# Contiguous copies, transposes as matmuls, and a coefficient moved to GpSimd in a metaformer block

## Time and profile before

| | us |
|---|---|
| median of the runs | 225.13 |
| the profiled execution | 225.83 |
| its span, first to last instruction | 223.9 |
| TensorE busy | 199.1 (89%) |
| ACT busy | 127.7 (57%) |
| DVE busy | 124.9 (56%) |
| GpSimd busy | 51.6 (23%) |

### The profile page before, as it was taken

The page is one execution under the profiler, slowest core; times in us unless marked ns, Lnnn a source line. Parts: engine busy times, 40 slices in busy tenths (PEclk is TensorE's granted clock), DMA queues, the critical chain, the costliest instruction groups (busy, mean ns, idle before and its releaser), DMA issues.

```text
span 223.9 us, 6080 instructions
## 1 busy us (share of the span) xinstructions
PE 199.1 (89%) x2674; PEld 103.9 (46%) x2674; DVE 124.9 (56%) x231; ACT 127.7 (57%) x207; POOL 51.6 (23%) x54
## 2 busy tenths in 40 slices
PE   7769688799994977659899999999999999999992
PEld 3546478453352857656234344444444444444430
DVE  0594076937949697699843643355433455333554
ACT  2349942014436725738887667866678666687630
POOL 5190393008599960040021000000000000000000
PEclk9999999999999599988999999999999999999998
DMA  6991000000000000000008852540706416071001
GB/s 213 272 260 32 3 3 6 4 0 3 0 3 1 0 3 3 6 3 3 0 12 194 195 144 48 138 97 3 187 0 140 97 41 148 3 180 54 3 0 47
DMA packets 6601, 14.27 MB, mean 64 GB/s; under 512 B 2736, under 2 KB 4144, under 8 KB 5680
## 3 DMA queue, kind: packets, MB, share of 16 engines
q1 hardware_dynamic: 6576, 13.89, 25.4%
HBM read 12.71 MB, written 1.18 MB: 62 GB/s over the span
## 4 chain that ended last, share of the span: by engine, by line
PE 76%; DVE 12%; ACT 7%; issue 3%; POOL 1%; DVEq 0%; POOLq 0%
PE psum L730 25%; PE psum L712 25%; PE psum L555 7%; PE psum L432 2%; PE psum L529 2%; PE psum L565 2%; PE psum L616 1%; DVE place L1063 1%; PE psum L662 1%; PE psum L515 1%; DVE place L1007 1%; DVE st L1003 1%; PE psum L584 1%; PE psum L475 1%; ACT hid L881 1%
## 5 line engine op out<-in xcount | busy, mean ns | idle before, releaser
L712 PE MATMUL psum<-tok,w1s 128*64 128x512 f16 x512 | 60.8, 381 | 1.2 <-ACT hid L881 0.5
L1186 DVE SCALAR_TENSOR_TENSOR term<-psum,sm,wide 128x512 f32<-128x512 f32 x32 | 24.0, 751 | 55.1 <-PE psum L730 52.6
L881 ACT ACTIVATE hid<-psum,b1p 128x512 f32<-128x512 f32 x64 | 38.5, 699 | 15.1 <-PE psum L712 14.8
L712 PEld LDWEIGHTS psum<-tok,w1s 128*64 128x64 f16 x512 | 27.5, 110 | 36.1 <-issue 8.8
L730 PE MATMUL psum<-hid,w 128*64 128x512 f32 x128 | 29.0, 592 | 0.0
L881 ACT ACTIVATE w1f<-psum,b1p 128x512 f32<-128x512 f32 x32 | 19.5, 687 | 15.2 <-PE psum L712 14.9
L1191 DVE TENSOR_TENSOR x<-x,term 128x512 f32<-128x512 f32 x32 | 22.1, 692 | 1.1
L881 ACT ACTIVATE w1g<-psum,b1p 128x512 f32<-128x512 f32 x32 | 19.6, 712 | 0.3
L555 PE MATMUL psum<-h_pad,tap_bd 64*64 64x512 f32 x144 | 15.9, 590 | 0.0
L730 PEld LDWEIGHTS psum<-hid,w 128*64 128x64 f32 x128 | 9.0, 137 | 14.9 <-issue 9.0
L730 PE MATMUL psum<-w1f,w 128*64 128x512 f32 x64 | 15.1, 592 | 0.0
(11 more groups left out here) (147 smaller groups left out, 287.5 us busy)
## 6 DMA issues: line engine op xcount, KB each, us to landing
wide<-gate_store SPq DMA_DIRECT2D x14, 512.0 KB, 6.4
xs<-in_x SPq DMA_DIRECT2D x2, 512.0 KB, 3.9
w1f<-in_W SPq DMA_DIRECT2D x2, 512.0 KB, 10.0
block_out<-x SPq DMA_DIRECT2D x4, 256.0 KB, 6.2
wide<-gate_store SPq DMA_DIRECT2D x2, 384.0 KB, 5.6
hid<-in_W1T SPq DMA_DIRECT2D x1, 512.0 KB, 10.5
w<-in_W SPq DMA_DIRECT2D x1, 512.0 KB, 11.8
sm<-in_small SPq DMA_DIRECT2D x1, 407.0 KB, 7.8
```

The lines of the kernel that those rows point to most:

```text
L712: mm = pe.matmul(h_bank(tile)[side * H:(side + 1) * H, :], w1s[:, part, e, k * P + side * H:k * P + (side + 1) * H], tok[:, pair, half, b, :],
L881: act.activation(hid_of[u % 4][:, B2 * k + b, :], h_bank(tile), ACT.Gelu, bias=b1p[:, e * KT + k:e * KT + k + 1]).then_inc(gelu_ready, 1)
L1186: dve.scalar_tensor_tensor(term[:, u % 2, :], y_bank(u), b2t[:, e:e + 1], gate_b[part][:, e % (E // 2), :], ALU.add, ALU.mult).then_inc(te ...
```

## The change

1. The ACT copies `keep_dw`, `keep_xd` and `keep_back` no longer rearrange what they copy. `keep_xd` and `keep_back` copy a bank as it lies; `keep_dw` writes runs of eight values. The rearrangement is done by TensorE: `dct_over_w` and `windows` write their results to PSUM with eight f32 values between neighbouring columns, `to_frequencies` reads its stationary operand with that distance, and `inverse_over_kh` reads its own with a distance of 16. The channels lie in another order in x's and x1's columns (`by_side`), and the cosine matrices for that axis have their columns or rows permuted.
2. The transposes `windows`, `places`, `heads` and `to_frequencies` are 32 quarter matmuls with the identity instead of eight 128x128 transposes, and each raises its semaphore once, at its end, where it did so after each half. `times_wv` waits for both copied banks, where it began with the first.
3. The low branch's coefficient is applied to its input: GpSimd multiplies `xd` by `coef` into a new tile `low_in` (`scale_low_in`, four operations of 512 columns for the two pairs), and `low` reads it. The bias, times `coef`, is a new tile `coef_bias` (one operation at the start) which GpSimd adds to `rest` (one more operation for each bank in `rest_ahead`, four in all). `mix_branches` on DVE is then one contiguous addition for each bank, where it was an operation with bias and coefficient and a rearranging addition.
4. The order of all engines is new (`TURN`, `UPS`, `DOWNS`, `GELUS`, `ADDS`). On TensorE `gram_matrices(0)` comes before `conv_in(1)`, `conv_in(0)` before `dct_over_w(1)`, `heads(0)` before `conv_out(1)`, and pair 0's inverse transform before `low(1)`; `down` of unit 0 comes after three `up`. On DVE `residual(0)` comes before `mix_branches(1)`. On GpSimd `weights_of_first` comes after the two `scale_low_in`.
5. Functions `other_*` can share a copy between ACT and DVE; `SHARED` is zero for all, so none issues anything. The gates are stored in pieces of 64 values where it was 128.

```
 TURN = {
+    "scale_low_in": (1, 2), "router_weights": (3, 4), "keep_router_weights": (5, 6), "weights_of_first": (3, 11),
+    "dct_over_h": (1, 2), "square_columns": (1, 2), "dct_over_w": (5, 8), "windows": (6, 10), "conv_in": (7, 12),
+    "keep_dw": (3, 8), "keep_xd": (4, 10), "gelu_in": (7, 11), "norm_columns": (1, 3), "places": (9, 13),
+    "keep_xt": (9, 12), "join": (4, 6), "rest_ahead": (5, 8), "high": (7, 9), "gram_matrices": (11, 15),
+    "gram_times_w": (14, 16), "norms": (17, 18), "mask_gram": (7, 9), "taps": (19, 22), "logits": (20, 24),
...
+    "gelu_out": (18, 22), "conv_out": (23, 28), "project": (26, 30), "exponent": (16, 20), "heads": (27, 33),
+    "times_wv": (29, 35), "keep_y": (19, 23), "low": (31, 37), "mask_mix": (20, 22), "keep_yt": (21, 25),
+    "to_frequencies": (32, 39), "inverse_over_kh": (34, 41), "keep_back": (24, 28), "keep_half": (26, 29),
+    "square_tokens": (27, 36), "mix_branches": (21, 24), "inverse_over_kw": (36, 42), "high_part": (30, 42),
+    "tokens": (38, 44), "residual": (23, 26), "norm_tokens": (25, 29), "keep_tokens": (31, 49), "features": (43, 58),
+    "low_part": (10, 12), "router": (40, 54), "route": (27, 32), "gates_to_rows": (52, 61), "shares": (28, 33),
...
+UPS = (45, 46, 47, 49, 50, 51, 53, 55, 57, 59, 60, 62)
+DOWNS = (48, 56)
+GELUS = (32, 33, 34, 37, 38, 39, 40, 43, 44, 46, 47, 50)
+ADDS = (34, 35)
...
 def dct_over_w(p):
-                    mm = pe.matmul(slot(p, 1)[rows_of(b), by_half(cp, side)], dh[p][rows_of(side), by_half(cp, b)], dct_w[rows_of(side)],
+                    to = bank(slot(p, 1), side).rearrange("p (m c) -> p c m", c=CP)[rows_of(b), cp]
+                    mm = pe.matmul(to, dh[p][rows_of(side), by_half(cp, b)], dct_w[rows_of(side)], start=True, stop=True)
...
 def windows(p):
-                    mm = pe.transpose(slot(p, 0)[:, k2 * P:(k2 + 1) * P], dw[p][:, k2 * P:(k2 + 1) * P], ident)
+                for k2, side, b in quarters():
+                    mm = pe.matmul(phase(slot(p, 0), b, k2)[rows_of(side)],
+                                      dw[p][rows_of(b), by_side(k2, side)], half_ident[rows_of(b)], start=True, stop=True)
...
 def low(p):
+                        pe.wait_ge(low_in_ready, 2 * p + g // K + 1)
-                                       xd[p][rows_of(half), g * H:(g + 1) * H], start=True, stop=True)
+                                       low_in[p][rows_of(half), g * H:(g + 1) * H], start=True, stop=True)
...
 def keep_xd(p):
-                    act.copy(xd[p].rearrange("p (n k) -> p k n", k=K)[:, 4 * j:4 * j + 4],
-                             bank(slot(p, 0), j).rearrange("p (k n) -> p k n", n=P)).then_inc(xd_ready, 1)
+                    act.copy(bank(xd[p], j), bank(slot(p, 0), j)).then_inc(xd_ready, 1)
...
 def scale_low_in(p):
+                for b in range(B2):
+                    pool.tensor_tensor(bank(low_in[p], b), bank(xd[p], b), coef, ALU.mult).then_inc(low_in_ready, 1)
 def rest_ahead(p):
+                    link(pool.tensor_tensor(bank(rest[p], b), bank(rest[p], b), coef_bias[:, :], ALU.add))
...
 def mix_branches(p):
-                    link(dve.scalar_tensor_tensor(bank(low_term[p], b), bank(slot(p, 1), b), weight("proj_b"), coef, ALU.add, ALU.mult))
-                    dve.tensor_tensor(x_out[p].rearrange("p (k b n) -> p b k n", k=K, b=B2)[:, b],
-                                      bank(low_term[p], b).rearrange("p (n k) -> p k n", k=K),
-                                      bank(rest[p], b).rearrange("p (n k) -> p k n", k=K), ALU.add).then_inc(xout_ready, 1)
+                    dve.tensor_tensor(bank(x_out[p], b), bank(slot(p, 1), b), bank(rest[p], b), ALU.add).then_inc(xout_ready, 1)
```

More of the change, by code:

```diff
@@ L43 @@
 TURN = {
[L44 to L53, removed]
@@ L198, in by_side, with phase, sided, others_of @@
         def by_side(chunk, side):
-            return slice(chunk * P + side * H, chunk * P + (side + 1) * H)
-        def by_half(chunk, half):
-            return slice(half * CHUNK + chunk * H, half * CHUNK + (chunk + 1) * H)
+            return slice(side * CHUNK + chunk * H, side * CHUNK + (chunk + 1) * H)
+        by_half = by_side
+        def phase(v, b, k2):
+            return bank(v, b).rearrange("p (n k) -> p k n", k=K)[:, k2]
+        def sided(v, side):
+            return v.rearrange("p (m s c) -> p s m c", s=2, c=CP)[:, side]
+        def others_of(name, p):
+            return sum(SHARED[name][:p + 1])
+        def banks_of(name, p):
+            return 2 * (p + 1) - others_of(name, p)
+        def banks(name, p):
+            return range(2 - SHARED[name][p])
         def rows_of(half):
@@ L255, in metaformer @@
         h_pad = sb("h_pad", [P, PAIRS, B2, H + 2, K + 2])
-        place = [sb(f"place{n}", [P, PAIRS, N]) for n in range(6)]
+        place = [sb(f"place{n}", [P, PAIRS, N]) for n in range(7)]
         wide = [sb(f"wide{n}", [P, PAIRS, 2 * N]) for n in range(2)]
@@ L260, in metaformer @@
         row = sb("row", [P, PAIRS, 3, HEADS * G])
-        gates = sb("gates", [P, PAIRS, 2, B2, E, TT // 2])
+        gates = sb("gates", [P, PAIRS, B2, E, TT])
         xd = [place[0][:, p, :] for p in range(PAIRS)]
         xc = xd
+        low_in = [place[6][:, p, :] for p in range(PAIRS)]
         squares = [place[1][:, p, :] for p in range(PAIRS)]
@@ L782, in keep_xt @@
             def keep_xt(p):
-                for j in range(2):
-                    act.wait_ge(xt_done, 2 * p + j + 1)
+                act.wait_ge(xt_done, p + 1)
+                for j in banks("xt", p):
                     act.copy(bank(xt[p], j), bank(slot(p, 1), j)).then_inc(xt_ready, 1)
@@ L961, in weights_of_first @@
                 pool.tensor_tensor(w1s[:, 1, :, :], w1g[:, :, :], w1s[:, 0, :, :], ALU.subtract).then_inc(w1_ready, 1)
-            for stage, (p,) in in_turn((weights_of_first, join, rest_ahead, high, low_part)):
+            for stage, (p,) in in_turn((weights_of_first, scale_low_in, join, rest_ahead, high, low_part)):
                 stage(p)
```

166 lines of the change are left out of this document (98 added, 68 removed).

## The result

Over 20 runs of each on one chip the kernel after has a median of 223.67 us (222.41 to 225.46) and the kernel before 225.67 us (223.81 to 229.28): a ratio of 0.992, with a 95% interval of 0.990 to 0.995. All ratios here leave out executions more than 1.5% above the fastest of the same kernel, so they aren't quite the quotients of the medians. Half a per cent to one per cent was won; 1.8% was forecast. The profiled execution took 223.29 us with a span of 221.5 us, against 225.83 and 223.9 us: 2.4 us less, not 4.2.

A forecast was written before the change was run, and what follows sets the result against it. TensorE's expert loop is busy without a hole, so time is won only before it, along the chain of waits: -1.8 - 1.8 - 0.2 - 0.8 + 0.4 = -4.2 us, giving 221.0 us, range 218.0 to 225.0 us.

The forecast's parts named there:

- the front's -1.8 us: 12 to 42 us: cheaper copies and the new order start `gram_times_w(0)` at 27.85 us instead of 29.62.
- Late instructions, the rival of 13%: 448 more matmuls make TensorE wait for issue, one to two stalls: +1.5 to +3, 222.5 to 224.0 us; 13%.
- 72 to 83 us, -1.8: `times_wv` to `mix_branches(0)`: earlier start, clock falling again, one shorter addition a bank; `x_out` complete at 79.6, not 83.16 us.
- the rival of 22%: The clock does not fall at 72 us: `times_wv` to `low(0)` end 2.3 us sooner, 218.6 us in all; 22%.
- "I take nothing": Strided TensorE operands and PSUM results: between nothing and 1.0 us a stage, 0 to 7 us in all, priced at nothing.
- the rival of 15%: Strided stationary reads cost 1.0 us each in `to_frequencies(0)` and `inverse_over_kh(0)`, half for pair 1: +3, 224.0 us; 15%.
- strided PSUM results: `dct_over_w` and `windows` writing PSUM eight apart: priced at nothing; rival (10%) had strided writes cost as well, 228.0 us.
- Tokens(1) at full clock, -0.8: Behind `features(0)`: the new order fills the 2.32 us hole, so `tokens(1)` takes 1.1 us instead of 1.94.
- First `up` to loop, +0.4: Was 20.3 us: ACT's squares for pair 1 add 1.1 us, the earlier `down(0)` gives some 0.7 back.

The follow-up runs named there:

- the repeat: The kernel after run again with no edit, against the kernel before: 224.50 us, 0.991 (0.987 to 0.995).
- the best version: The kernel after with contiguous stationary operands and 2 and 3 idle matmuls instead of 6 and 6, against the kernel before: 221.29 us, 0.982.

## Why the prediction was wrong, step by step

The medians show 2.0 us won where 4.1 were forecast. Two terms of the sum failed: the front's -1.8 us, of which 0.1 came, and the strided stationary operands, put at nothing, which cost 1.0 and 0.85 us a stage. One piece of luck hid part of it: the clock did not fall at 72 us. For that case the prediction's own sum is 218.6 us, 5 us below the measured median.

- **Front, -1.8 us at `gram_times_w(0)`: failed.** It came 0.1 us earlier, though `dct_over_w(0)` itself had started 0.7 earlier. ACT's copies were priced rightly. From `dct_over_w(0)` to `gram_times_w(0)` I had 15.8 us; the kernel before took 17.6, and the kernel after and its variants took 17.4 to 18.6 in the nine profiles without added idle matmuls. I had carried over from the earlier trace rows that pair 0's stages run at full clock, but in all these nine half clock was granted somewhere between 10 and 24 us. Then either the idle matmuls (1.2 us longer) or the stages themselves take the copies' gain; with 12, 5 or none of them the ratio is the same within its interval. My count left the idle matmuls out altogether. The two profiles with added idle matmuls had full clock there and took 17.7 and 18.1 us, of which 1.6 and 1.7 were late instructions: 16.1 and 16.4 without these, near the forecast. The old layouts hid the half clock: the kernel before with eight and five idle matmuls more behind this stretch had it from 12 to 15 us and took 17.7 us, where it took 17.6 at full clock.
- **The new order may cost at the front, which I didn't count.** With the old layouts in the new order the same stretch took 18.5, 18.6 and 19.0 us, against 17.6 and 17.7 in the old order (21.5 in the long execution of the coefficient part alone). Against the new order's three, the new layouts with their 17.4 to 18.6 win some tenths to 1 us, and the order takes it back. The clock differs between these profiles too, so this is argued and not shown.
- **Where it is missing in the profile.** Of 1.65 us (29.50 against my 27.85), 0.9 stand already at `conv_in(0)`, 17.93 us instead of 17.0, behind the idle matmuls. Another 0.4 come in `dct_over_w(1)`, 1.53 us at full clock and 1.16 in the repeat, and the rest in `windows(1)`, which has 0.47 us of late instructions.
- **Late instructions, the rival of 13%: in part.** 3.3 us instead of 1.8 in the first profile, 2.5 in the repeat, but 1.7 with 5 idle matmuls instead of 12 and as many instructions otherwise. That their removal isn't won in the median (0.997 with 224 fewer matmuls) stays unexplained.
- **72 to 83 us, -1.8: right for `mix_branches`, the rest luck.** `times_wv(0)` started at 73.72 us, 0.9 later than before, where I had 71.5. From there to the end of `low(0)` it took 4.5 us instead of 6.8, since the clock did not fall (the rival of 22%; it stayed full there in six of the nine profiles): 2.3 us, as the rival had it. Then `mix_branches(0)`, at 0.69 us a bank as priced, won the 2.8 us that I had given it. So it ended 4.2 us earlier, not 3.6; had the clock fallen, it would by these numbers have been 1.9. The hole before `times_wv(0)` was 1.97 us, not the 2.4 that I had counted.
- **"I take nothing" for strided operands: failed for the stationary ones.** 2.16 and 2.01 us for the stages, so 1.0 and 0.85 us each for pair 0, and 1.5 us between `mix_branches(0)` and `norm_tokens(0)`, net of ACT's saving. Pair 1's two stages lie on the chain as well. This was the rival of 15%, at +3 us; taking the stride away gave 1.55 and 2.0 us in the two pairs of medians on one chip each, and only the second pair's intervals don't meet. My reason, that each of four quarter matmuls side by side has four times 18 ns, does not hold for its stationary operand: its load went from 135 to 213 and 200 ns.
- **For strided PSUM results "nothing" was right**: 1.16 us either way, and once more when `to_frequencies` was made to write strided. The Trainium skill ("Advanced Engine Details and Errata", section "Memory Cachelines") had been the reason to fear them, and no run here agrees. For SBUF the same section of the Trainium skill asks for at least two hits on each 16-byte line; stationary operands 32 and 64 bytes apart have one, and these runs agree with it. I quoted the Trainium skill for PSUM and did not weigh its rule for SBUF where it bore on two stages of the path.
- **Tokens(1) at full clock, -0.8: right in the stage, not on the path.** It took 1.16 us against 1.94, but from `norm_tokens(0)` to the first `up` nothing was won: 10.4 us against 10.0, with pair 1's strided stages on the chain. In the repeat the clock fell at 95 us.
- **First `up` to loop, +0.4: right**, 20.6 us against 20.3.
- **The sum.** -4.2 forecast. The profiles show -2.3 at the first `up`: -4.2 up to 78.9 us (+0.9 at `times_wv(0)`, -2.3 from the clock, -2.8 from `mix_branches`), +1.5 from the strides, +0.4 from 90 us on, where ACT was still with pair 1's later `keep_half`. The run with both costs reduced, contiguous stationary operands and 5 idle matmuls, has 0.982, the ratio that I had forecast, and needs two edits more for it.
- **How far the clock goes.** Of the 20 executions of the kernel after one was granted full clock throughout. It took 223.92 us, 0.25 above the median: half clock alone doesn't explain what is missing.
- **What carries it.** The coefficient part alone gives 0.989, with the new order 0.988, with layouts too 0.991 to 0.992; these intervals overlap, so the rest of the change has not been shown to add anything. The three parts don't add: order alone 1.013, layouts and coefficient in the old order 1.006. I had summed the three on one path; the front's gain, which I put down to layouts and order, is what is missing.

## What to carry to other kernels

When a layout change takes a stride away from ACT's and DVE's copies and gives it to TensorE, try it on the result in PSUM before the stationary operand: in these stages of 64 f32 quarter matmuls the one was free and the other cost 0.85 to 1.0 us on 1.16. Before a saving of a microsecond in a stretch of short waits is counted, look at the clock of that stretch in more than one execution, as one profile's full clock may be luck. What a part of a change is worth depends on the order of the stages around it (the new order alone lost 1.3%, and with the coefficient part it lost nothing), so try each part in the order that it will have.

## What was not expected of the hardware

- A stage of 64 quarter matmuls with transposing stationary reads took 2.16 us strided and 1.16 us contiguous; the stage after it 2.01 and 1.16 us. A weight load took 213 and 200 ns instead of 135.
- The runs of the kernel before spread over 5.5 us (223.8 to 229.3), those of the kernel after over 3.0 us and of the best version over 2.2 us (6 runs): the lowest differ by 1.4 us, the highest by 3.8, so a part of what was won is in the worst runs, and no profile shows it.
- Idle matmuls added in holes of the kernel after cost 4 us of the median (0.991 to 1.010) though each stood where TensorE had waited; half clock came elsewhere and instructions came 1.6 and 1.9 us late. In the kernel before, such matmuls in two of the three places cost nothing (0.994). Idle matmuls taken out cost nothing either: 0.991 with 5 instead of 12.
